# Attention block with a following linear layer, eight cores: the K and V evacuations of the first stage are issued three tiles later

## The chip, the cores and the metric

One Trainium2 chip; all 8 of its cores run the same program, each on one element of a batch of 8. The metric is the device time in microseconds (us) of the slowest core. Engines are named as the profile names them: PE is TensorE (matmuls; PEld its weight loads), DVE VectorE, ACT ScalarE, POOL GpSimd, SP SyncE, whose queue issues DMAs.

## The reference, cut to what matters

For each of 8 batch elements x of 2048 rows (tokens) by 2048 columns:

```python
def layer(x):
    a = layernorm(x)                                   # over the last axis
    q = einsum('bpd,hde->bphe', a, W_Q) + b_Q          # 16 heads of 128; k and v alike
    scores = where(causal, q @ k.T / sqrt(128), -1e5)
    z = softmax(scores) @ v
    x = x + layernorm(einsum('bqhe,hed->bqd', z, W_O) + b_O)
    w = where(weight >= 0, 1, -1) * mean(abs(weight))  # mean over each output row
    return x + layernorm(layernorm(x) @ w.T + bias)
```

## The kernel before, in words

The kernel is written as a list of instructions for each engine (class `Plan`). `p.op(engine, ...)` appends one instruction to that engine's list, with semaphore waits ahead of it; an engine works through its own list in order, so the order of the Python code is the order of the work. Every instruction that others wait for raises its engine's counter (PE, DV, SC, GP), and a wait names a value of such a counter.

The program has these parts in a row:

- **Stage A** (loop `for t in range(NT + 2)`, ahead of line 401): the first layernorm of 16 tiles of 128 tokens, transposed into `arena_a` (`ln1t3`), and the Q, K and V projections of head 0. `emit_A_head(t)` loads tile t of x into one of four buffers `xa` (the issue is at L240, on SP for even and on POOL for odd tiles; it waits until tile t-4 was normalized), takes its statistics on DVE (`emit_ln_stats`: four BATCH_NORM_STATS2 at L210 and one aggregate at L213) and its 1/std on ACT (`emit_rstd`, L221 and L225). `emit_A_tail(t)` normalizes on DVE (L256; the page shows its output as `v` or `ptil`, the two halves of a double buffer), transposes 16 blocks on PE into psD and psE (L270), and copies them out on ACT (L276). The loop runs head(t) and then tail(t-2). After the tails of tiles 3, 7, 11 and 15 a slice of 512 tokens is complete, and `emit_w_mms(0, wi, only_slice=s)` is called for Q, K and V (wi 0, 1, 2): 16 matmuls each (L366) and one evacuation each on DVE (L380), which adds the bias and writes `qt`, `kt` or `vstage` (shown as `ptil`). Q and V of slice s use one bank of psA or psB, K one half of psC. The waits of the matmuls are counter values kept in `dv_qkv_evac_d[(h, wi)]`.
- **Heads**: for each of 16 heads the bound for the softmax (`emit_mh_sq`, `emit_mh_mms`, `emit_mh_tail`: L476 to L526), the transposed V (L574), scores (L604), exponentials (L618), masks, normalization, and the product with V (L691). Q of the next head is computed beside the last group of a head, K and V (still `emit_w_mms`, for whole heads, four slices at a time) at the start of the next.
- **Weights** of the linear layer: binarized and transposed, and then the output projection, the two later layernorms and the linear layer, tile by tile (from `emit_bw_tile` on).

The first instruction that needs all of stage A is the DVE multiplication at L476 (`emit_mh_sq(0, 0)`), which stands right behind the last evacuation in DVE's list.

Of the kernel before, what the change touches and what calls it, by code (L numbers as in the profile page):

```python
# [10 lines left out]
ALU = mybir.AluOpType  # L11
# [49 lines left out]
def build_program(SEQ, DM, H):  # L61
# [3 lines left out]
    SLW = min(512, SEQ)  # L65
# [11 lines left out]
    p = Plan(nc)  # L77
# [32 lines left out]
    bqkvT_sb = nc.alloc_sbuf_tensor("bqkvT_sb", [128, 3 * H], F32)  # L110
# [63 lines left out]
    for dst, src in ((eye_sb, eye_h), (tri_sb, tri_h), (onec_sb, onec_h),  # L174
# [3 lines left out]
             inc="CONST", incn=16)  # L178
# [56 lines left out]
    def emit_A_head(t):  # L235
        slot = t % 4
        par = t % 3
        wait = [("DV", dv_apply[t - 4])] if t - 4 in dv_apply else []
        xt = p.op(("sync", "gpsimd")[slot % 2], lambda e, sl=slot, t=t:
                  e.dma_start(xa[sl], x_h.ap()[t * 128:(t + 1) * 128, :]),  # L240
                  wait=wait, inc=XAs[slot], incn=16)
        xa_tot[slot] = xt
        aggr = emit_ln_stats(xa[slot], par, [(XAs[slot], xt)],
                             war_sc=sc_rstdA.get(t - 3, 0))
        sc_rstdA[t] = emit_rstd(par, aggr, war_dv=dv_apply.get(t - 3, 0))
# [44 lines left out]
    dv_bank_free = 0  # L290
# [18 lines left out]
    dv_qkv_evac_d = {}  # L309
    dv_qkv_evac_s = {}  # L310
# [6 lines left out]
    pe_bw_par = [0, 0]  # L317
    pe_bw_tr = {}

    def emit_w_mms(h, wi, only_slice=None):  # L320
        nonlocal dv_bank_free
        bankset = [[psD[:, 0:SLW], psE[:, 0:SLW], psC[:, 0:SLW],
                    psC[:, 512:512 + SLW]],
                   [psA[:, 0:SLW], psA[:, 512:512 + SLW], psB[:, 0:SLW],
                    psB[:, 512:512 + SLW]]]
        sidx = 0 if wi == 1 else 1
        banks = bankset[sidx]
        slot = (3 * h + wi) % 4
        dst = (qt_sb[:], kt_sb[:], vstage)[wi]
        tpsl = NT // NSL  # L330
        pe_mm = 0
        if only_slice is not None:
            slices = [(only_slice, 1)]
        else:
            slices = [(sq0, min(4, NSL - sq0)) for sq0 in range(0, NSL, 4)]
        for sq0, nq in slices:
            for c in range(NCH):
                wait = []
                if c == 0:
                    wait = [(WSs[slot], ws_t[(h, wi)])]  # L340
                    if only_slice is not None:
                        wait.append(("DV", dv_qkv_evac_d.get((h, wi), 0)))
                    if sidx == 0:
                        wait += [("DV", dv_zevac.get(gidx - 1, 0)),
                                 ("DV", dv_mbias_prev),
                                 ("SC", sc_rinv_prev),
                                 ("SC", max(sc_bw_evac_half)),
                                 ("DV", dv_qkv_evac_d.get((h, 0), dv_bank_free))]
                    else:
                        wait += [("SC", max(psbuf_last_rd)),  # L350
                                 ("DV", dv_vch.get(h - 1, 0)),
                                 ("DV", dv_red_last)]
                        if wi == 2:
                            wait.append(("DV", dv_qkv_evac_d.get((h, 0), 0)))
                for k in range(nq):
                    s = sq0 + k
                    w = list(wait) if k == 0 else []
                    if c == 0:
                        w.append(("SC", sc_evacA[min((s + 1) * tpsl, NT) - 1]))
                    w = w or ()  # L360
                    bidx = (2 + s % 2) if (only_slice is not None and wi == 1) \
                        else (s % 4)
                    tgt = p.op(
                        "tensor", lambda e, c=c, s=s, sl=slot, banks=banks,
                        bidx=bidx:
                        e.matmul(banks[bidx],  # L366
                                 wslot[sl][:, c * 128:(c + 1) * 128],
                                 ln1t3[:, c, s * SLW:(s + 1) * SLW],
                                 start=(c == 0), stop=(c == NCH - 1)),
                        wait=w,  # L370
                        inc="PE" if (c == NCH - 1 and k == nq - 1) else None)
            pe_mm = tgt
            for k in range(nq):
                s = sq0 + k
                bidx = (2 + s % 2) if (only_slice is not None and wi == 1) \
                    else (s % 4)
                dv_bank_free = p.op(
                    "vector", lambda e, s=s, d=dst, wi=wi, h=h, banks=banks,
                    bidx=bidx:
                    e.tensor_scalar(d[:, s * SLW:(s + 1) * SLW], banks[bidx],  # L380
                                    bqkvT_sb[:, wi * H + h:wi * H + h + 1],
                                    None, ALU.add), wait=[("PE", pe_mm)],
                    inc="DV")
                dv_qkv_evac_s[(h, wi, s)] = dv_bank_free
        if (h, wi) in pe_w_done_d:
            pe_mm = max(pe_mm, pe_w_done_d[(h, wi)])
            dv_bank_free = max(dv_bank_free, dv_qkv_evac_d[(h, wi)])
        pe_w_done_d[(h, wi)] = pe_mm
        pe_w_done[(h, wi)] = pe_mm
        dv_qkv_evac_d[(h, wi)] = dv_bank_free  # L390

    sc_evacA = {}
    for t in range(NT + 2):
        if t < NT:
            emit_A_head(t)
        if t - 2 >= 0:
            emit_A_tail(t - 2)
            tp = t - 2
            if (tp + 1) % (NT // NSL) == 0 and H > 0:
                s = (tp + 1) // (NT // NSL) - 1  # L400
                for wi in range(3):
                    emit_w_mms(0, wi, only_slice=s)

    sc_ln1t_all = sc_evacA[NT - 1]

# [136 lines left out]
    for h in range(H):  # L542
        if h > 0:
            emit_w_mms(h, 1)
            emit_mh_sq(1, h)
            emit_w_mms(h, 2)
# [6 lines left out]
        if h >= wo_start:  # L553
# [3 lines left out]
            for hh in range(hh0, min(hh0 + per, H)):  # L557
                p.op("gpsimd", lambda e, hh=hh: e.dma_start(
                    Bz[:, hh * DM:(hh + 1) * DM], wo_h.ap()[hh]),
                    inc="WO", incn=16)  # L560
# [8 lines left out]
        wait = [("DV", dv_qkv_all), ("DV", dv_mx_d[1])]  # L569
        nh = NT // 2  # L570
        pe_vtr_half = 0
        for t in range(NT):
# [4 lines left out]
                inc="PE" if t in (nh - 1, NT - 1) else None)  # L577
# [3 lines left out]
        for j in range(max(SEQ // GQ, 1)):  # L581
# [3 lines left out]
            wait=[("PE", pe_vtr_half)], inc="DV")  # L585
        dv_vch[h] = p.op("vector", lambda e, nh=nh: e.tensor_copy(
            v_sb[:, nh * 128:NT * 128], psA_bf[:, nh * 128:NT * 128]),
            wait=[("PE", pe_vtr)], inc="DV")
# [46 lines left out]
        for g in range(NG):  # L635
            chunks = (g + 1) * TPG
            gp_mask_j = {}
            for r in range(TPG):
                j = g * TPG + r
                if r > 0:  # L640
                    p.op("gpsimd", lambda e, j=j, r=r: e.memset(
                        ptil[:, j * GQ:j * GQ + r * 128], 0.0),
                        wait=[("SC", sc_exp[j])], inc="GP")
# [5 lines left out]
            for j in range(chunks):  # L649
                wait = [("SC", sc_exp[j])] if j < g * TPG else \  # L650
                    [("GP", gp_mask_j[j])]
                if j == 0:
# [4 lines left out]
                    wait=wait, inc="PE" if j == chunks - 1 else None)  # L657
# [7 lines left out]
                wait=[("DV", rbc_war[g % 2])], inc="SC",  # L665
# [3 lines left out]
            for j in range(chunks):  # L669
                wait = [("SC", sc_rinv)] if j == 0 else []  # L670
                if j == 0:
# [3 lines left out]
                    wait=wait, inc="DV")  # L675
# [10 lines left out]
            for j in range(chunks):  # L686
                wait = [("DV", dv_norm[j])]
                if j == 0:
# [5 lines left out]
                    wait=wait, inc="PE")  # L694
                ptil_slot_av[j] = pe_av
            pe_av_all[h] = pe_av
            if g + 1 < NG:
# [8 lines left out]
            wait = [("PE", pe_av), (ZWs[zpar], zw_par_t[zpar])]  # L706
# [6 lines left out]
                wait=[("DV", dv_zevac[gidx])], inc=ZWs[zpar], incn=16)  # L713
# [249 lines left out]
    for i in range(NT):  # L963
# [6 lines left out]
        if i > 0:  # L970
# [5 lines left out]
         wait=[("OUT0", p.cnt("OUT0"))])  # L976
# [14 lines left out]
def _get_nc():  # L991
    key = (_SEQ, _DM, _H)
    if key not in _nc_cache:
        _nc_cache[key] = build_program(*key)
    return _nc_cache[key]
# [30 lines left out]
```

How the kernel before makes its waits and increments, by code:

```python
        def thunk(e, fn=fn, wait=wait, inc=inc, incn=incn, lowp=lowp):  # L43
            for (s, v) in wait:
                e.wait_ge(sems[s][0], v)
            if lowp is not None:
                with nc.allow_low_precision(reason=lowp):
                    ins = fn(e)
            else:
                ins = fn(e)
            if inc is not None:
                ins.then_inc(sems[inc][0], incn)
```

## Time and profile before

| what | us |
|---|---|
| median of 3 runs | 2348.21 (2347.74 to 2537.95) |
| the profiled execution, its own time | 2351.13 |
| its span on the slowest core (core 0) | 2349.3 |
| spans of the eight cores | 2335.3 to 2349.3 |
| stage A of core 0: first statistics to the multiplication at L476 | 17.9 to 182.1 |

The span is the time from the first to the last instruction of a core. All times in the rows are read from the span's start, on core 0 unless a row names another. "Idle before" and the arrow say how long an engine stood still ahead of an instruction, and what released it.

### The profile page before, as it was taken

What the parts mean: (1) busy time and instruction counts of PE and PEld (TensorE: products, weight loads), DVE (VectorE), ACT (ScalarE), POOL (GpSimd) and SP (SyncE); (2) the same over time, 40 slices, a digit from 0 to 9 for tenths busy, and PEclk for the clock granted to TensorE, in tenths of its full rate; (3) what the DMA queues carried; (4) which work ended last, traced back from release to release, by engine and by line L of the source; (5) the groups of instructions that cost most, each with busy time, mean ns of one, the idle gap of its engine ahead of it and who ended that gap; (6) DMA issues with size and microseconds to landing.
All of it is one profiled execution on the core that took longest, in us unless ns stands there. A gap on an engine that the chain in (4) does not pass through costs nothing.

```text
span 2349.3 us, 27218 instructions; the slowest of 8 cores (2335.3 to 2349.3 us)
## 1 busy us (share of the span) xinstructions
PE 1859.7 (79%) x8180; PEld 803.8 (34%) x8336; DVE 938.5 (40%) x1712; ACT 613.9 (26%) x785; POOL 240.3 (10%) x558
## 2 busy tenths in 40 slices
PE   1556887879788797887978878787855899999995
PEld 1232333323233242333423333233323344444442
DVE  3443433333333333332333323333345455555553
ACT  1234041230413314032140321404256211111111
POOL 1001021110111101011010111111010000000000
PEclk9768998989889898898988989899876899999997
DMA  6232212212122131121312233252044223333320
GB/s 154 90 82 24 30 17 22 26 16 30 16 23 26 14 32 16 21 27 14 32 16 21 27 50 31 44 65 46 5 141 177 58 71 87 90 90 90 90 81 36
DMA packets 178475, 119.34 MB, mean 51 GB/s; under 512 B 168100, under 2 KB 168100, under 8 KB 170148
## 3 DMA queue, kind: packets, MB, share of 16 engines
q0 software_dynamic: 107200, 75.51, 18.2%
q1 hardware_dynamic: 71140, 42.07, 7.2%
q8 instruction: 79, 1.29, 0.2%
q14 instruction: 56, 0.46, 0.1%
HBM read 125.97 MB, written 25.17 MB: 64 GB/s over the span
## 4 chain that ended last, share of the span: by engine, by line
PE 64%; ACT 10%; DVE 8%; issue 8%; POOL 4%; DMA 4%; DVEq 2%; ACTq 0%; POOLq 0%; another core or an unknown queue 0%; SPq 0%
PE psA L366 10%; PE psB L366 10%; PE psE L691 8%; ACT ptil L618 6%; PE psC L366 5%; PE psC L890 5%; PE psB L781 5%; PE psA L781 5%; PE psC L654 3%; POOL ptil L644 2%; PE psE L890 2%; PE psD L890 2%; PE psD L366 2%; PE psE L366 2%; DMA c<-x 2%
## 5 line engine op out<-in xcount | busy, mean ns | idle before, releaser
L673 DVE TENSOR_TENSOR ptil<-ptil,c 128x512 bf16<-128x512 bf16 x640 | 220.2, 417 | 479.9 <-ACT c L663 473.8
L366 PE MATMUL psA<-arena_a,wbuf 128*128 128x512 bf16 x1002 | 299.3, 384 | 6.8 <-ACT arena_a L276 3.8
L366 PE MATMUL psB<-arena_a,wbuf 128*128 128x512 bf16 x1002 | 298.4, 383 | 5.0 <-ACT arena_a L276 4.0
L691 PE MATMUL psE<-ptil,v 128*128 128x512 bf16 x625 | 187.8, 394 | 53.4 <-DVE ptil L673 53.1
L654 PE MATMUL psC<-ptil,onem_sb 128*128 128x512 bf16 x624 | 181.3, 402 | 53.8 <-POOL ptil L644 24.8
L618 ACT ACTIVATE ptil<-psA,mbias 128x1024 bf16<-128x1024 f32 x160 | 178.3, 1114 | 166.9 <-PE psE L691 80.1
L508 ACT ACTIVATE srow<-srow 1x1 f32<-1x1 f32 x32 | 6.5, 202 | 808.5 <-DVE srow L503 808.5
L644 POOL TENSOR_TENSOR ptil<-ptil,tri_sb 128x128 bf16<-128x128 bf16 x256 | 108.8, 425 | 861.4 <-ACT ptil L618 861.3
L618 ACT ACTIVATE ptil<-psB,mbias 128x1024 bf16<-128x1024 f32 x160 | 177.2, 1107 | 0.0
L890 PE MATMUL psC<-arena_a,c 128*128 128x512 bf16 x496 | 149.7, 381 | 17.7 <-DVE c L874 9.3
L366 PE MATMUL psC<-arena_a,wbuf 128*128 128x512 bf16 x538 | 156.6, 380 | 4.9 <-DVE qt L380 4.5
L604 PE MATMUL psA<-qt,kt 128*128 128x512 bf16 x314 | 109.1, 423 | 59.7 <-ACT ptil L618 49.4
L366 PEld LDWEIGHTS psA<-arena_a,wbuf 128*128 128x128 bf16 x1024 | 101.0, 99 | 130.9 <-issue 15.7
L366 PEld LDWEIGHTS psB<-arena_a,wbuf 128*128 128x128 bf16 x1024 | 100.9, 99 | 125.4 <-issue 8.4
L604 PE MATMUL psB<-qt,kt 128*128 128x512 bf16 x315 | 108.9, 430 | 25.9 <-ACT ptil L618 25.5
L691 PEld LDWEIGHTS psE<-ptil,v 128*128 128x128 bf16 x640 | 62.2, 97 | 187.1 <-issue 152.7
L654 PEld LDWEIGHTS psC<-ptil,onem_sb 128*128 128x128 bf16 x640 | 63.1, 99 | 175.2 <-issue 126.9
L890 PE MATMUL psE<-arena_a,c 128*128 128x512 bf16 x256 | 97.5, 381 | 0.1
L890 PE MATMUL psD<-arena_a,c 128*128 128x512 bf16 x255 | 97.1, 381 | 0.0
L366 PE MATMUL psD<-arena_a,wbuf 128*128 128x512 bf16 x235 | 89.5, 381 | 4.6 <-issue 3.2
L366 PE MATMUL psE<-arena_a,wbuf 128*128 128x512 bf16 x231 | 88.0, 381 | 0.3
L380 DVE TENSOR_SCALAR kt<-psD,bqkvT_sb 128x512 bf16<-128x512 f32 x15 | 11.3, 751 | 190.8 <-PE psC L366 190.8
(131 smaller groups left out, 2128.9 us busy)
## 6 DMA issues: line engine op xcount, KB each, us to landing
c<-fw POOLq DMA_DIRECT2D x16, 1024.0 KB, 6.3
ptil<-x SPq DMA_DIRECT2D x16, 1024.0 KB, 6.8
out<-wbuf POOLq DMA_DIRECT2D x16, 1024.0 KB, 9.4
wbuf<-wq POOLq DMA_DIRECT2D x16, 512.0 KB, 7.2
wbuf<-wk POOLq DMA_DIRECT2D x16, 512.0 KB, 7.1
c<-x SPq DMA_DIRECT2D x8, 1024.0 KB, 5.2
wbuf<-wv POOLq DMA_DIRECT2D x16, 512.0 KB, 7.1
zs<-c SPq DMA_DIRECT2D x64, 128.0 KB, 1.9
```

Source lines behind the costliest of these rows:

```text
L366: e.matmul(banks[bidx], wslot[sl][:, c * 128:(c + 1) * 128], ln1t3[:, c, s * SLW:(s + 1) * SLW], start=(c == 0), stop=(c == NCH - 1)),
L380: e.tensor_scalar(d[:, s * SLW:(s + 1) * SLW], banks[bidx], bqkvT_sb[:, wi * H + h:wi * H + h + 1], None, ALU.add), wait=[("PE", pe_mm)],
L508: t_ln = p.op("scalar", lambda e, wh=which: e.activation(srow[0:1, 18 + wh:19 + wh], srow[0:1, 16 + wh:17 + wh], AF.Ln, bias=0.0, scale=1. ...
L604: pe_sc[j] = p.op("tensor", lambda e, j=j, g=g, hb=hb: e.matmul(schalf[hb], kt_sb[:, j * 128:(j + 1) * 128], qt_sb[:, g * GQ:(g + 1) * GQ] ...
L618: t_exp = p.op("scalar", lambda e, buf=buf, dst=dst: e.activation(dst, buf, AF.Exp, bias=mbias[:, 0:1], scale=C_ATTN), wait=wait, inc="SC")
L644: gp_mask_j[j] = p.op("gpsimd", lambda e, j=j, r=r: e.tensor_tensor(ptil[:, j * GQ + r * 128:j * GQ + (r + 1) * 128], ptil[:, j * GQ + r * ...
L654: pe_den = p.op("tensor", lambda e, j=j, chunks=chunks: e.matmul(psC[:, 512:512 + GQ], onem_sb[:], pslot[j], start=(j == 0), stop=(j == ch ...
L673: dv_norm[j] = p.op("vector", lambda e, j=j, g=g: e.tensor_tensor(pslot[j], pslot[j], rbc[g % 2], ALU.mult), wait=wait, inc="DV")
L691: pe_av = p.op("tensor", lambda e, j=j, chunks=chunks: e.matmul(psE[:, 0:GQ], v_sb[:, j * 128:(j + 1) * 128], pslot[j], start=(j == 0), st ...
L781: p.op("tensor", lambda e, hh=hh, s=s, d=zrd: e.matmul(projb[s], d[:, hh * 128:(hh + 1) * 128], Bz[:, hh * DM + s * 512:hh * DM + s * 512 ...
L890: p.op("tensor", lambda e, c=c, s=s: e.matmul(ffnb[s], ln3t[:, c * 128:(c + 1) * 128], bwt3[:, c, s * 512:s * 512 + PSW], start=(c == 0), ...
```

## The change

`emit_w_mms` gets an argument `defer_evac`. With it the function issues the matmuls but not the DVE evacuations; it returns a function that issues them and only then records their counter value in `dv_qkv_evac_d`. Stage A now calls it like this: matmuls of Q, matmuls of K, evacuation of Q, matmuls of V; the evacuations of K and V are issued three tiles later, after the tail of tile tp+3 (tiles 6, 10 and 14), and those of the last slice after the loop. Because Q's evacuation of the same slice isn't recorded yet when K's matmuls are issued, their wait on `dv_qkv_evac_d[(h, 0)]` names the evacuation of the slice before. The calls for heads 1 to 15 don't defer.

```diff
-    def emit_w_mms(h, wi, only_slice=None):
+    def emit_w_mms(h, wi, only_slice=None, defer_evac=False):
...
+        deferred = []
...
-            for k in range(nq):
-                s = sq0 + k
...
-                dv_bank_free = p.op(
...
+            def do_evacs(sq0=sq0, nq=nq, pe_mm=pe_mm, banks=banks):
+                nonlocal dv_bank_free
+                for k in range(nq):
...
+                    dv_bank_free = p.op(
...
+            if defer_evac:
+                deferred.append(do_evacs)
+            else:
+                do_evacs()
         if (h, wi) in pe_w_done_d:
             pe_mm = max(pe_mm, pe_w_done_d[(h, wi)])
-            dv_bank_free = max(dv_bank_free, dv_qkv_evac_d[(h, wi)])
         pe_w_done_d[(h, wi)] = pe_mm
         pe_w_done[(h, wi)] = pe_mm
-        dv_qkv_evac_d[(h, wi)] = dv_bank_free
+
+        def finish():
+            nonlocal dv_bank_free
+            for f in deferred:
+                f()
+            cur = dv_qkv_evac_d.get((h, wi), 0)
+            dv_qkv_evac_d[(h, wi)] = max(cur, dv_bank_free)
+        if defer_evac:
+            return finish
+        finish()
 
     sc_evacA = {}
+    wA_flush = {}
     for t in range(NT + 2):
         if t < NT:
             emit_A_head(t)
         if t - 2 >= 0:
             emit_A_tail(t - 2)
             tp = t - 2
+            for f in wA_flush.pop(tp, ()):
+                f()
             if (tp + 1) % (NT // NSL) == 0 and H > 0:
                 s = (tp + 1) // (NT // NSL) - 1
-                for wi in range(3):
-                    emit_w_mms(0, wi, only_slice=s)
+                flq = emit_w_mms(0, 0, only_slice=s, defer_evac=True)
+                flk = emit_w_mms(0, 1, only_slice=s, defer_evac=True)
+                flq()
+                flv = emit_w_mms(0, 2, only_slice=s, defer_evac=True)
+                wA_flush[tp + 3] = [flk, flv]
+    for fl in sorted(wA_flush):
+        for f in wA_flush[fl]:
+            f()
```

DVE before, from the normalization of tile 3 (output `ptil`) to the head of tile 9; `qt`, `kt` and `ptil` at L380 are the evacuations of Q, K and V of slice 0:

```order
L256 TENSOR_SCALAR ptil<-ptil,mv2_0,rstd_0 128x2048
L380 TENSOR_SCALAR qt<-psA,bqkvT_sb 128x512
L380 TENSOR_SCALAR kt<-psC,bqkvT_sb 128x512
L380 TENSOR_SCALAR ptil<-psA,bqkvT_sb 128x512
L210 BN_STATS st6_0<-c2 128x6 x4
L213 BN_AGGR mv2_0<-st6_0 128x2
L256 TENSOR_SCALAR v<-c2,mv2_1,rstd_1 128x2048
L210 BN_STATS st6_1<-ptil 128x6 x4
L213 BN_AGGR mv2_1<-st6_1 128x2
L256 TENSOR_SCALAR ptil<-c2,mv2_2,rstd_2 128x2048
```

The same place after the change, down to the deferred pair:

```order
L256 TENSOR_SCALAR ptil<-ptil,mv2_0,rstd_0 128x2048
L384 TENSOR_SCALAR qt<-psA,bqkvT_sb 128x512
L210 BN_STATS st6_0<-c2 128x6 x4
L213 BN_AGGR mv2_0<-st6_0 128x2
L256 TENSOR_SCALAR v<-c2,mv2_1,rstd_1 128x2048
L210 BN_STATS st6_1<-ptil 128x6 x4
L213 BN_AGGR mv2_1<-st6_1 128x2
L256 TENSOR_SCALAR ptil<-c2,mv2_2,rstd_2 128x2048
L210 BN_STATS st6_2<-c2 128x6 x4
L213 BN_AGGR mv2_2<-st6_2 128x2
L256 TENSOR_SCALAR v<-c2,mv2_0,rstd_0 128x2048
L384 TENSOR_SCALAR kt<-psC,bqkvT_sb 128x512
```

The evacuations of K and V moved from ahead of the statistics of tile 6 to behind the normalization of tile 6, that is past the statistics of tiles 6, 7 and 8 and the normalizations of tiles 4, 5 and 6 (V's follows K's there).

DVE at the end of stage A, before, from the normalization of tile 13 to the multiplication at L476:

```order
L256 TENSOR_SCALAR ptil<-c2,mv2_1,rstd_1 128x2048
L256 TENSOR_SCALAR v<-c2,mv2_2,rstd_2 128x2048
L256 TENSOR_SCALAR ptil<-ptil,mv2_0,rstd_0 128x2048
L380 TENSOR_SCALAR qt<-psB,bqkvT_sb 128x512
L380 TENSOR_SCALAR kt<-psC,bqkvT_sb 128x512
L380 TENSOR_SCALAR ptil<-psB,bqkvT_sb 128x512
```

And after the change:

```order
L256 TENSOR_SCALAR ptil<-c2,mv2_1,rstd_1 128x2048
L256 TENSOR_SCALAR v<-c2,mv2_2,rstd_2 128x2048
L384 TENSOR_SCALAR kt<-psC,bqkvT_sb 128x512
L384 TENSOR_SCALAR ptil<-psB,bqkvT_sb 128x512
L256 TENSOR_SCALAR ptil<-ptil,mv2_0,rstd_0 128x2048
L384 TENSOR_SCALAR qt<-psB,bqkvT_sb 128x512
```

Here the pair of slice 2 stands ahead of the normalization of tile 15; the pair of slice 3 follows Q's as before.

PE's list has the same instructions in the same order. What changes there is a wait, shown for slice 0; before:

```order
L366 MATMUL psA<-arena_a,wbuf 128x512 [waits WS0,SC]
L366 MATMUL psA<-arena_a,wbuf 128x512 x15
L366 MATMUL psC<-arena_a,wbuf 128x512 [waits WS1,DV,SC]
L366 MATMUL psC<-arena_a,wbuf 128x512 x15
L366 MATMUL psA<-arena_a,wbuf 128x512 [waits WS2,DV,SC]
```

after:

```order
L367 MATMUL psA<-arena_a,wbuf 128x512 [waits WS0,SC]
L367 MATMUL psA<-arena_a,wbuf 128x512 x15
L367 MATMUL psC<-arena_a,wbuf 128x512 [waits WS1,SC]
L367 MATMUL psC<-arena_a,wbuf 128x512 x15
L367 MATMUL psA<-arena_a,wbuf 128x512 [waits WS2,DV,SC]
```

K's first matmul no longer waits for DVE in slice 0; in slices 1 to 3 a DVE wait stays, for an evacuation of the slice before.

## Rows read from the trace of the kernel before

**Rows 1.** The page: the span, busy times, and the granted clock in 40 slices.

```profile
span 2349.3 us, 27218 instructions; the slowest of 8 cores (2335.3 to 2349.3 us)
PE 1859.7 (79%) x8180; PEld 803.8 (34%) x8336; DVE 938.5 (40%) x1712; ACT 613.9 (26%) x785; POOL 240.3 (10%) x558
...
PEclk9768998989889898898988989899876899999997
```

**Rows 2.** By stretch: length, busy PE, PEld, DVE, ACT, POOL, clock, DMA share, GB/s.

```profile
17.89:60.60 42.71, 7.46 (x64) 6.51 (x65) 21.55 (x34) 12.26 (x21) 1.06 (x2) 1.00 0.61 159
...
61.00:75.50 14.50, 12.52 (x47) 4.92 (x46) 2.25 (x4) 0.00 (x0) 0.00 (x0) 1.00 0.06 26
...
75.50:98.60 23.10, 7.46 (x64) 6.64 (x66) 16.14 (x25) 9.98 (x16) 1.06 (x2) 0.57 0.49 165
...
182.00:2349.00 2167.00, 1781.31 (x7736) 758.46 (x7888) 865.22 (x1605) 572.69 (x720) 227.75 (x538) 0.92 0.24 46
```

**Rows 3.** Timeline of slice 0: PE and DVE (start, us, engine, instruction, idle before).

```profile
61.01 5.45 PE L366 MATMUL psA<-arena_a,wbuf 128*128 128x512 bf16 x15 [1.92 <-ACT arena_a L276]
...
66.57 0.75 DVE L380 TENSOR_SCALAR qt<-psA,bqkvT_sb 128x512 bf16<-128x512 f32 x1 [9.70 <-PE psA L366]
...
67.57 3.61 PE L366 MATMUL psC<-arena_a,wbuf 128*128 128x512 bf16 x16 [1.11 <-DVE qt L380]
...
71.02 3.62 PE L366 MATMUL psA<-arena_a,wbuf 128*128 128x512 bf16 x16
...
74.75 0.75 DVE L380 TENSOR_SCALAR ptil<-psA,bqkvT_sb 128x512 bf16<-128x512 f32 x1 [2.70 <-PE psA L366]
...
75.42 2.46 DVE L210 BATCH_NORM_STATS2 st<-c 128x6 f32<-128x512 f32 x4
```

**Rows 4.** Timeline of tiles 4 to 7, to the start of slice 1.

```profile
78.45 1.35 DVE L256 TENSOR_SCALAR v<-c,mv,rstd 128x2048 bf16<-128x2048 f32 x1 [0.23 <-issue]
...
80.16 1.01 PE L270 MATMUL psD<-eye_sb,v 128*128 128x128 bf16 x8 [5.52 <-DVE v L256]
...
84.65 0.53 POOL L240 DMA_DIRECT2D c<-x  x1 [26.70 <-DVE ptil L256]
...
85.09 2.47 DVE L210 BATCH_NORM_STATS2 st<-c 128x6 f32<-128x512 f32 x4 [1.00 <-DMA c<-x]
...
88.14 1.35 DVE L256 TENSOR_SCALAR v<-c,mv,rstd 128x2048 bf16<-128x2048 f32 x1 [0.23 <-issue]
...
90.15 2.47 DVE L210 BATCH_NORM_STATS2 st<-c 128x6 f32<-128x512 f32 x4 [0.67 <-DMA c<-x]
...
98.67 1.91 PE L366 MATMUL psA<-arena_a,wbuf 128*128 128x512 bf16 x4 [1.92 <-ACT arena_a L276]
```

**Rows 5.** Timeline of slices 1 to 3: the rows that differ or set a term.

```profile
127.65 0.69 DVE L210 BATCH_NORM_STATS2 st<-c 128x6 f32<-128x512 f32 x1 [0.74 <-DMA c<-x]
...
161.93 1.35 DVE L256 TENSOR_SCALAR ptil<-ptil,mv,rstd 128x2048 bf16<-128x2048 f32 x1 [0.76 <-PE psE L270]
...
164.78 0.61 PE L270 MATMUL psD<-eye_sb,ptil 128*128 128x128 bf16 x8 [0.46 <-ACT arena_a L276]
...
168.59 4.58 PE L366 MATMUL psB<-arena_a,wbuf 128*128 128x512 bf16 x15 [2.06 <-ACT arena_a L276]
...
182.12 1.22 DVE L476 TENSOR_TENSOR c<-qt 128x2048 bf16<-128x2048 bf16 x1
```

**Rows 6.** Chain that ended last, 40 to 100 us: the longest DMA piece.

```profile
45.59 6.73 DMA c<-x
```

**Rows 7.** Waits of PE, 17 to 182 us (total, times, longest).

```profile
PE psC L366 <- DVE qt L380: 4.5, 4, 1.1
```

**Rows 8.** Span and granted clock by core: the two that bear on the price of clock.

```profile
core 2: 2345.1 us, clock 0.914
...
core 5: 2337.1 us, clock 0.922
```

More of the change, by code:

```diff
@@ L372, in emit_w_mms @@
             pe_mm = tgt
-            for k in range(nq):
-                s = sq0 + k
-                bidx = (2 + s % 2) if (only_slice is not None and wi == 1) \
-                    else (s % 4)
-                dv_bank_free = p.op(
[L378 to L384, printed above, removed]
+            def do_evacs(sq0=sq0, nq=nq, pe_mm=pe_mm, banks=banks):
+                nonlocal dv_bank_free
+                for k in range(nq):
+                    s = sq0 + k
+                    bidx = (2 + s % 2) if (only_slice is not None and
+                                           wi == 1) else (s % 4)
+                    dv_bank_free = p.op(
+                        "vector", lambda e, s=s, d=dst, wi=wi, h=h,
+                        banks=banks, bidx=bidx:
+                        e.tensor_scalar(d[:, s * SLW:(s + 1) * SLW],
+                                        banks[bidx],
+                                        bqkvT_sb[:, wi * H + h:
+                                                 wi * H + h + 1],
+                                        None, ALU.add),
+                        wait=[("PE", pe_mm)], inc="DV")
+                    dv_qkv_evac_s[(h, wi, s)] = dv_bank_free
+            if defer_evac:
+                deferred.append(do_evacs)
+            else:
+                do_evacs()
         if (h, wi) in pe_w_done_d:
             pe_mm = max(pe_mm, pe_w_done_d[(h, wi)])
-            dv_bank_free = max(dv_bank_free, dv_qkv_evac_d[(h, wi)])
         pe_w_done_d[(h, wi)] = pe_mm
         pe_w_done[(h, wi)] = pe_mm
-        dv_qkv_evac_d[(h, wi)] = dv_bank_free
+        def finish():
[7 more added lines that the diff above has]
+        finish()
     sc_evacA = {}
+    wA_flush = {}
     for t in range(NT + 2):
```

## The prediction, made before the changed kernel ran

> **What bounds the kernel now.** I read the page first: PE is busy for 79% of the span and nothing else is above 40% [rows 1]. That is a mean over parts with different limits, so it says nothing of stage A, the only part in which the change reorders work. So I asked for busy times by stretch next. From 17.89 to 182 us PE is mostly idle: 7.46 us busy of 42.71, and 7.46 of 23.10 between slices 0 and 1, while DVE is busy for 16.14 of those 23.10 [rows 2]. In the stretch with the projection matmuls it is the other way round: PE 12.52 us of 14.50, DVE 2.25 [rows 2]. The two engines take turns. The reader should see that stage A is a chain that passes from one to the other.
>
> The timeline says why. The three evacuations of a slice stand ahead of the statistics of the next tile in DVE's list, so DVE must wait for all 48 matmuls. For slice 0 Q's evacuation starts at 66.57, V's at 74.75, and only at 75.42 do the statistics of tile 6 begin [rows 3]. Their row shows no wait of its own for data. From then on DVE is the chain: normalization of tile 4 at 78.45, of tile 6 at 88.14, statistics of tile 9 at 90.15 (with short waits for loads: 1.00 and 0.67 us), and slice 1 starts on PE at 98.67 [rows 4]. PE waited 5.52 us for the normalized tile 4 [rows 4]. Everything behind stage A begins with the multiplication at 182.12 [rows 5], and no later instruction is tied to anything but its predecessors, so what stage A gains should arrive at the end.
>
> **The change, term by term.**
>
> *Statistics of tiles 6, 10 and 14 come earlier.* They used to follow V's evacuation and now follow Q's. The distance is 74.75 - 66.57 = 8.18 us in slice 0 [rows 3], and the matmul counts, so the distance too, are the same in slices 1 and 2. The data is there: tile 6 was loaded long before, and the row at 75.42 shows no wait [rows 3]. So the normalization of tile 4 should start at 78.45 - 8.18 = 70.27, that of tile 6 at 79.96.
>
> *The loads of tiles 8 and 9.* Each is issued when DVE has normalized tile 4 or 5 and frees the buffer, so both issues move up by the same 8.18 us, at the same distance from each other. The chain of tiles 4 to 6 keeps its rhythm, the wait of 1.00 us before the statistics of tile 8 included [rows 4]. The load issued at 84.65 is awaited until 90.15, 5.5 us later [rows 4]. The slowest such piece in the chain is 6.73 us, where more loads were in flight [rows 6]; the stretch without loads has room for them (DMA share 0.06 at 61.00:75.50) [rows 2]. Two loads a block that took 6.73 instead would cost some 1.3 us each in blocks 0 and 1: at most 5 us, and I take 0, since the spacing is that of the rows.
>
> *The deferred evacuations.* Two of them now stand between the normalization of tile 6 and the statistics of tile 9. One takes 75.42 - 74.75 = 0.67 us of DVE back to back [rows 3], so 1.34 us. By then the matmuls of K and V are long done. Before, DVE stood idle at that point for 0.67 us (slice 0) and 0.74 us (slice 1), waiting for a load [rows 4, 5], and the evacuations fill that. The cost is 1.34 - 0.67 = 0.67 and 1.34 - 0.74 = 0.60 us. Block 0 then gains 7.51 us and block 1 7.58; slice 1 would start at 98.67 - 7.51 = 91.16.
>
> *Behind slice 2* the pair stands ahead of the normalization of tile 15. Before, that waited 0.76 us for PE [rows 5], and its transposes, 164.78, waited for ACT's copies [rows 5], 164.78 - (161.93 + 1.35) = 1.50 us after it was done. So 2.26 us of slack stand against 1.34 us: nothing, and the block keeps the whole 8.18 us.
>
> *PE behind the matmuls of V.* The transposes of tile 4 are queued on PE behind V's matmuls, which end at 71.02 + 3.62 = 74.64 [rows 3], less 1.11 by the next term: 73.5. The tile itself would be ready at 70.27 + 1.35 = 71.6. They start 2 us late, and end about 2.1 us on (two groups like the 1.01 us one [rows 4]), at 75.6. What needs them is ACT's copy and the normalization of tile 6 at 79.96, so this costs nothing; PE would have to be over 4 us later before it did. In the last block the same holds for tile 12: ready 2 us late, awaited by the normalization of tile 14, which also waits for tile 13's on DVE.
>
> *K's wait for Q's evacuation goes.* Before each group of K matmuls PE waited 1.11 us for it, 4.5 us in all four slices [rows 3, 7], though K uses another bank. In slices 0 to 2 the end of V's matmuls is no longer in the chain, so nothing comes of it. In slice 3 DVE waits for all three groups and then goes on to the multiplication: 1.11 us. V's wait for Q's evacuation stays, but that is done 0.85 us after Q, and V's turn comes 3.5 us after.
>
> The skill has a rule beside this row. The Trainium skill, "Perfetto Trace Analysis", section "Matmuls", says that independent groups should rotate through PSUM banks so that one's evacuation overlaps the next one's matmuls, and its section "Optimization Strategy" warns that a gap that keeps coming back can mean too little room in SBUF or PSUM. The first is what the removed wait allows. The second would speak against the change, which holds the banks of K and V longer; here the next group to use each is at least a slice away and the gap would be zero, so the sum is the same by either.
>
> *Removed and added instructions.* None on any engine. Heads 1 to 15 issue the same lists with the same waits: zero.
>
> *Sum.* 7.51 + 7.58 + 8.18 + 1.11 = 24.4 us. The profiled execution took 2351.13 us, so 2326.7 beside it. It is 2.9 us above the median of the runs, 2348.21; against that, 2348.2 - 24.4 = 2323.8. I predict 2324 us. That is 1.0%, below the 2% that a measurement of this kernel can tell from no change.
>
> **The clock.** The granted clock swings between its two levels, 1.2 and 2.4 GHz. Q's 16 matmuls (one record is missing) take 5.45 us in slice 0 and 4.58 in slice 3, against 3.61 for K's 16 at the higher level [rows 3, 5]. Where PE had been idle between transposes, the mean is 0.57 [rows 2]. After the change PE's pauses have other lengths. If Q's matmuls always ran at the higher level, slices 1 and 2 would each save some 1.9 us more and slice 3 1.0: 5 us. If they all ran at the lower level, 16 matmuls would take twice 3.5, 7.0 us: 1.5 us more in each of two slices and 2.4 in slice 3, 5.4 us lost. I take zero, the row nearest: three transposed tiles and a pause stand before Q as before.
>
> The Trainium skill, "TensorE: Matmul & The Clock Gate", section "Part 1: The HAM clock gate", states that how many slow matmuls a kernel shows differs between runs of the same kernel, since the gate isn't in step with the program. By that rule Q's time isn't decided by the code at all and could come out at either bound; 5.45 against 4.58 us in one trace agrees. It gives the two clock cases below.
>
> **The rivals.**
>
> *A, the forecast:* DVE's chain moves up, 2324; its own range is 2316 to 2332 (clock and loads as bounded above, and the median's own spread).
>
> *B, the clock helps:* denser work on PE keeps Q at the higher level: 2324 - 5 = 2319. For it: the transposes of tile 15 took 0.61 us instead of 1.01 where PE had been busy [rows 4, 5]. Against it: after them slice 3 still began slowly.
>
> *C, the clock or the loads take some of it:* 2324 + 5 = 2329. For it: the one load of 6.73 us [rows 6].
>
> *D, the shift is absorbed:* something in the heads starts at its old time. 2348. Against it: the chain of stage A ends in the multiplication and nothing in the rows stands still beside it.
>
> *E, slower:* stage A gains but the later parts, 2167 us with a granted clock of 0.92 [rows 2], start at another phase and get a lower clock. Two cores of one run price that: 0.914 with 2345.1 and 0.922 with 2337.1 us [rows 8], 1 us for each 0.001. The gain is used up at a clock lower by 0.024, at 0.892, and from there it is slower; at 0.88 it would be 2324 + 36 = 2360. Against it: no core shows under 0.914.
>
> *F, a larger gain:* the same mechanism the other way, the clock at 0.94 and above: 2324 - 24 = 2300.
>
> *G, the wait doesn't go:* K's matmuls of slice 3 would still wait 1.11 us if the recorded value were the same slice's. That is 2325, inside A's range, and only the trace would tell.
>
> **How the numbers follow.** A with G 0.72, B 0.08, C 0.08, D 0.05, E 0.04, F 0.03. The time is A's. A's own range is 2316 to 2332; B and C lie in it, and with the unknown of the clock in the long part (4 to 6 us by the spread of the cores) I take 2312 to 2337. D, E and F are left out, 0.12. Faster by over 2% is F alone (2301 or less): 0.03. Slower by over 2% (2395 or more) is the far part of E, 0.02. The rest, 0.95, is within 2%.
>
> **What would show it.** Right: the statistics behind Q's evacuation start 0.7 us after it, without a wait; slice 1 begins near 91.2 us, the multiplication at L476's place near 157.7; DVE's waits for K's and V's matmuls are gone except in slice 3; PE has no idle time between Q and K in any slice; the loads are awaited as before. Wrong: a wait for a load of more than 1.5 us before the statistics of tile 8 (C); an earlier multiplication with an unchanged end (D); a stretch behind stage A that is not 2167 us long within some 5 us (E or F); a wait of DVE on PE at the deferred evacuations, which would say that the matmuls were late.

## The result, and the profile after

The changed kernel takes 2322.96 us (median of 8 executions) against 2348.75 us (also 8): the ratio is 0.9893, with a 95% interval of 0.9881 to 0.9905. That is 25 us less. 2324 us had been forecast, 24.4 us under the kernel before. In some executions of either kernel the cores of a die show a lower clock and take some per cent longer; ratios here, and every time given for an experiment below, are taken from the undisturbed executions alone (2322.62 us for the changed kernel by its 7, 2347.98 us for the one before by its 6).

The slowest core is now core 3. Its span and the two views that answer to [rows 1, 2]; the columns of the stretches are as there:

```profile
span 2320.3 us, 27373 instructions; the slowest of 8 cores (2309.2 to 2320.3 us)
PE 1867.9 (81%) x8336; PEld 799.3 (34%) x8336; DVE 938.0 (40%) x1712; ACT 613.7 (26%) x785; POOL 240.2 (10%) x558
```

```profile
61.00:75.50 14.50, 12.49 (x68) 5.93 (x67) 8.73 (x13) 2.84 (x6) 0.00 (x0) 1.00 0.26 93
75.50:90.60 15.10, 4.61 (x48) 3.99 (x46) 9.39 (x14) 7.15 (x11) 1.06 (x2) 0.55 0.54 186
157.81:2320.30 2162.49, 1794.09 (x7888) 757.44 (x7888) 865.28 (x1605) 572.44 (x720) 227.65 (x538) 0.92 0.24 46
```

In the stretch with slice 0's matmuls DVE is busy for 8.73 us of 14.50 where it was 2.25 [rows 2]. The engines no longer only take turns. Slice 1 starts at 90.60 us, where on core 0 before the change it started at 98.67 [rows 4]. The busy times of DVE, ACT and POOL over the whole span are within 0.5 us of those before (PE's differ by the matmul records that the first trace lacks): no work was saved, only waiting.

The timeline of slice 0 and its four tiles, on core 3, which answers to [rows 3, 4]:

```profile
60.57 4.95 PE L367 MATMUL psA<-arena_a,wbuf 128*128 128x512 bf16 x16 [1.54 <-ACT arena_a L276]
65.35 3.62 PE L367 MATMUL psC<-arena_a,wbuf 128*128 128x512 bf16 x16
65.63 0.75 DVE L384 TENSOR_SCALAR qt<-psA,bqkvT_sb 128x512 bf16<-128x512 f32 x1 [8.82 <-PE psA L367]
66.30 2.46 DVE L210 BATCH_NORM_STATS2 st<-c 128x6 f32<-128x512 f32 x4
...
69.33 1.34 DVE L256 TENSOR_SCALAR v<-c,mv,rstd 128x2048 bf16<-128x2048 f32 x1 [0.23 <-issue]
...
72.26 0.61 PE L270 MATMUL psD<-eye_sb,v 128*128 128x128 bf16 x8
...
76.84 2.47 DVE L210 BATCH_NORM_STATS2 st<-c 128x6 f32<-128x512 f32 x4 [1.86 <-DMA c<-x]
...
79.88 1.35 DVE L256 TENSOR_SCALAR v<-c,mv,rstd 128x2048 bf16<-128x2048 f32 x1 [0.23 <-issue]
...
81.14 0.75 DVE L384 TENSOR_SCALAR kt<-psC,bqkvT_sb 128x512 bf16<-128x512 f32 x1
...
81.80 0.74 DVE L384 TENSOR_SCALAR ptil<-psA,bqkvT_sb 128x512 bf16<-128x512 f32 x1
...
82.46 2.46 DVE L210 BATCH_NORM_STATS2 st<-c 128x6 f32<-128x512 f32 x4
...
90.60 5.29 PE L367 MATMUL psA<-arena_a,wbuf 128*128 128x512 bf16 x16 [1.54 <-ACT arena_a L276]
```

The statistics of tile 6 begin 0.67 us after the start of Q's evacuation (8.85 us before the change, on core 0). K's matmuls follow Q's without idle time. The deferred pair stands at 81.14 with no wait ahead of it. The first transposes of tile 4, at 72.26, follow V's matmuls directly and take 0.61 us; before the change, after a pause of 5.52 us, they took 1.01.

Who waits for whom in stage A, 18.92 to 157.81 us, DVE's and PE's waits in total, times, longest; this answers to [rows 7] (most of the 37.7 us for loads lies ahead of slice 0; behind Q's first evacuation it is 3.7 us on this core):

```profile
DVE st L210 <- DMA c<-x: 37.7, 6, 18.9
DVE qt L384 <- PE psB L367: 18.9, 2, 9.5
DVE qt L384 <- PE psA L367: 18.0, 2, 9.2
DVE kt L384 <- PE psC L367: 2.7, 1, 2.7
DVE ptil L384 <- PE psB L367: 2.7, 1, 2.7
```

The wait of PE for Q's evacuation is no longer in PE's list. K's and V's evacuations wait once each, in slice 3. What is left on DVE is the wait for Q's matmuls in all four slices, 36.9 us.

To compare stages over all cores I read, on each core, when Q is evacuated in slices 0 to 3 and when the multiplication behind stage A begins. The three distances between the evacuations are blocks 0 to 2, the last distance is block 3; "behind" is the span less the start of the multiplication. Medians over the eight cores, in us:

| | block 0 | block 1 | block 2 | block 3 | first evacuation of Q to multiplication | behind |
|---|---|---|---|---|---|---|
| before | 37.49 | 37.50 | 31.58 | 8.84 | 115.55 | 2162.4 |
| after | 30.31 | 30.53 | 23.57 | 7.57 | 90.37 | 2159.2 |

Each block ends with Q's 16 matmuls of the next slice, and their time swings with the clock, from 3.7 to 6.7 us from core to core and run to run. So a second reading leaves them out: from the start of Q's evacuation to the start of the next slice's first matmul. Medians over the eight cores, in us, for runs described below:

| | block 0 | block 1 | block 2 |
|---|---|---|---|
| before | 31.60 | 31.57 | 26.51 |
| relaxed wait alone | 30.72 | 30.35 | 25.24 |
| one tile later | 26.03 | 25.93 | 20.57 |
| two tiles later | 23.79 | 23.41 | 18.95 |
| deferral with K's wait kept | 24.08 | 23.94 | 18.51 |
| after | 24.13 | 24.34 | 17.94 |
| after, second run | 23.85 | 24.05 | 17.92 |

### The profile page after: what moved, and what is told of

Read it like the earlier page. It is cut to its first block, busy times and chain, and to the rows that moved or that the text cites. A ratio compares the mean times of both kernels' runs of the same rounds, so it can differ in the third digit from the quotient of the medians.

```text
span 2320.3 us, 27373 instructions; the slowest of 8 cores (2309.2 to 2320.3 us)
## 1 busy us (share of the span) xinstructions
PE 1867.9 (81%) x8336; PEld 799.3 (34%) x8336; DVE 938.0 (40%) x1712; ACT 613.7 (26%) x785; POOL 240.2 (10%) x558
## 4 chain that ended last, share of the span: by engine, by line
PE 65%; ACT 10%; issue 8%; DVE 7%; POOL 4%; DMA 3%; DVEq 2%; ACTq 0%; POOLq 0%; SPq 0%
PE psB L367 10%; PE psA L367 9%; PE psE L718 8%; ACT ptil L645 6%; PE psC L917 5%; PE psA L808 5%; PE psB L808 5%; PE psC L367 5%; PE psC L681 3%; POOL ptil L671 3%; PE psD L917 2%; PE psE L917 2%; PE psD L367 2%; PE psE L367 2%; DMA c<-x 2%
## 5 line engine op out<-in xcount | busy, mean ns | idle before, releaser
L367 PE MATMUL psB<-arena_a,wbuf 128*128 128x512 bf16 x1024 | 303.9, 383 | 2.9 <-ACT arena_a L276 2.9
L681 PE MATMUL psC<-ptil,onem_sb 128*128 128x512 bf16 x640 | 183.4, 400 | 51.8 <-POOL ptil L668 24.8
```

What stands on the lines that cost most here:

```text
L367: e.matmul(banks[bidx], wslot[sl][:, c * 128:(c + 1) * 128], ln1t3[:, c, s * SLW:(s + 1) * SLW], start=(c == 0), stop=(c == NCH - 1)),
L681: pe_den = p.op("tensor", lambda e, j=j, chunks=chunks: e.matmul(psC[:, 512:512 + GQ], onem_sb[:], pslot[j], start=(j == 0), stop=(j == ch ...
```

## The experiments

**One part alone: K's wait relaxed, nothing deferred.**

```diff
                 flq()
-                flv = emit_w_mms(0, 2, only_slice=s, defer_evac=True)
-                wA_flush[tp + 3] = [flk, flv]
+                flk()
+                emit_w_mms(0, 2, only_slice=s)
```

> Undoes the deferral and keeps only the relaxed wait of K's matmuls. Theory (DVE's chain carries the gain): K's wait was on the path only in slice 3, but here DVE still waits for all three groups in every slice, so it is on the path four times: 4 x 1.1 to 1.3 = 4.4 to 5 us off, about 2344; the stretch from the first evacuation of Q to the multiplication at L476's place falls from 115.5 us to about 110.7. Rival (the removed wait, through PE's order and clock, carries most of the gain): 2330 or less. Rival (the wait costs nothing): 2348.7.

Measured: 2342.7 us against 2348.2 for the kernel before beside it, ratio 0.9988 (0.9963 to 1.0013). The interval leaves open whether anything was gained; one of the eight executions, at 2362.35 us, widens it, and the other seven lie at 2341.48 to 2345.45. The stretch is clear: it is 110.79 us instead of 115.55, and the blocks 36.78, 36.60, 30.96 and 7.57 us. Without Q's matmuls blocks 0 to 2 are 0.9, 1.2 and 1.3 us shorter, and block 3 is 1.3: the wait counted in all four, as expected, 4.6 us in all. On core 0 the wait moved into the evacuations' own lines:

```profile
66.92 0.75 DVE L384 TENSOR_SCALAR qt<-psA,bqkvT_sb 128x512 bf16<-128x512 f32 x1 [10.20 <-PE psA L367]
...
70.37 0.75 DVE L384 TENSOR_SCALAR kt<-psC,bqkvT_sb 128x512 bf16<-128x512 f32 x1 [2.70 <-PE psC L367]
...
73.82 0.75 DVE L384 TENSOR_SCALAR ptil<-psA,bqkvT_sb 128x512 bf16<-128x512 f32 x1 [2.70 <-PE psA L367]
```

DVE waits 2.70 us for K's and as long for V's matmuls. The theory that the relaxed wait carries most of the gain falls.

**The other part alone: deferral, with K's wait as it was.**

```diff
-                flq = emit_w_mms(0, 0, only_slice=s, defer_evac=True)
+                emit_w_mms(0, 0, only_slice=s)
                 flk = emit_w_mms(0, 1, only_slice=s, defer_evac=True)
-                flq()
```

> Keeps the deferral of K and V, but K's matmuls wait for Q's evacuation of their slice as before. Theory: only slice 3 is exposed to that wait, so 1.1 to 1.3 us slower than the changed kernel: about 2324, and the stretch from Q's first evacuation to the multiplication about 91.7 us against 90.4 (median of the cores) of the changed kernel. Rival (the wait matters in every slice): 4.5 to 5 us slower, 2328. Rival (the wait carries most of the gain): 2340 or more.

Measured: 2324.0 us, ratio 0.9903 (0.9874 to 0.9932). The blocks are 30.11, 30.31, 24.38 and 8.85 us. In blocks 0 and 1 the restored wait costs nothing, in block 3 it costs the 1.28 us that it had cost before (8.85 against 7.57). It also costs 0.57 us in block 2, which nobody had forecast: without Q's matmuls that block takes 18.51 us against 17.94, and the cores of the two kernels don't overlap. The rows show V's matmuls ending later and the transposes of tile 12 behind them starting later; that the end of block 2 hangs on them is read from this, not tested. The parts don't add up as if each stood alone: the relaxed wait is worth 4.6 us without the deferral and 1.9 us with it. The difference of this kernel to the changed one, 1.4 us in time, is within what the intervals can tell; the blocks show it.

**How much DVE waits for PE: only V deferred.**

```diff
                 flq()
+                flk()
                 flv = emit_w_mms(0, 2, only_slice=s, defer_evac=True)
-                wA_flush[tp + 3] = [flk, flv]
+                wA_flush[tp + 3] = [flv]
```

> Only V's evacuation is deferred; K's stays behind Q's, and DVE waits for K's 16 matmuls before the next tile. Theory (what counts is how long DVE stands still for PE): 3.45 us of each block's 8.18 come back, and one evacuation of 0.67 us less stands in the later place where it cost something in two blocks: 3 x (8.18 - 3.45) + 1.2 = 15.4 us under the kernel before, 2333.4; the stretch about 100 us. Rival (all or nothing, the loads set the pace once DVE is somewhat earlier): about 2323 as with both deferred. Rival (no gain while DVE still waits for PE): 2344 as with the relaxed wait alone.

Measured: 2333.25 us (median of three, 2330.60 to 2338.12), ratio 0.9944 (0.9916 to 0.9971). The stretch is 100.22 us where 100 had been expected, the blocks 33.30, 33.11, 27.59 and 7.57. The profiled execution is the one that took 2338.12 us, and its cores say why: six of them take 99.7 to 102.9 us, cores 6 and 7 take 105.4 and 105.3. On these two K's and V's 16 matmuls took 4.38 us (once 4.18), where K's took 3.62 on all others, and on core 6 DVE waited 3.45 us for K's instead of 2.70. Slice 0 on core 6:

```profile
66.55 4.38 PE L367 MATMUL psC<-arena_a,wbuf 128*128 128x512 bf16 x16
...
70.75 4.38 PE L367 MATMUL psA<-arena_a,wbuf 128*128 128x512 bf16 x16
...
71.04 0.75 DVE L384 TENSOR_SCALAR kt<-psC,bqkvT_sb 128x512 bf16<-128x512 f32 x1 [3.45 <-PE psC L367]
```

The granted clock over these two groups was 0.81 in slice 1 there, and 1.00 on core 0. Both other theories fall: the gain isn't all or nothing, and it doesn't need a DVE that never waits. With 3.45 of each block's 8.18 us of standing still given back, 15.3 of 25.2 us of gain are left in the stretch.

**Where the deferred pair goes: one tile later instead of three.**

```diff
-                wA_flush[tp + 3] = [flk, flv]
+                wA_flush[tp + 1] = [flk, flv]
```

> K and V are evacuated one tile after the slice instead of three, behind the normalization of tile 4, 8 and 12. Theory: V's matmuls end some 1.7 us after DVE gets there, so with the evacuations DVE loses about 2.6 us there, of which the wait for the load of tile 8 (1.9 us on the slowest core) hides most: 0.6 to 1.2 us a block, 2 to 4 us slower than the changed kernel, 2325 to 2327. Rival (the place three tiles later matters, since it is where DVE was idle): 6 to 8 us slower, 2330.

Measured: 2329.2 us, ratio 0.993 (0.9905 to 0.9955); the stretch is 96.69 us. By the stretch it is 6.3 us slower than the changed kernel, by the medians 6.6: the number of the rival. (By the ratios it would be 9, but that includes one execution of 2348.37 us, where the other six lie at 2326.70 to 2330.01.) The mechanism is the theory's, though, and the price was mis-sized. The blocks are 31.45, 31.03, 26.51 and 7.57 us: 1.1 and 0.5 us lost in blocks 0 and 1 and 2.9 in block 2. Without Q's matmuls, which happened to be faster in blocks 0 and 1 of this run, the losses are 1.9, 1.6 and 2.6 us. The timeline of block 2 on core 2, DVE:

```profile
134.10 1.35 DVE L256 TENSOR_SCALAR v<-c,mv,rstd 128x2048 bf16<-128x2048 f32 x1 [0.61 <-issue]
135.36 0.75 DVE L384 TENSOR_SCALAR kt<-psC,bqkvT_sb 128x512 bf16<-128x512 f32 x1
136.92 0.75 DVE L384 TENSOR_SCALAR ptil<-psB,bqkvT_sb 128x512 bf16<-128x512 f32 x1 [0.82 <-PE psB L367]
137.59 2.46 DVE L210 BATCH_NORM_STATS2 st<-ptil 128x6 f32<-128x512 f32 x4
```

DVE waits for V's matmuls (0.82 us here, 1.20 in block 0) and spends 137.59 - 135.36 = 2.23 us in the pair. In block 2 no core waits for a load, in this kernel or in the changed one, so no such wait hides any of it. I had charged every block as if one did, and in blocks 0 and 1 I had counted too much as hidden.

**Two tiles later, and the changed kernel once more.** The edit is `tp + 2` in the same line, and nothing.

> K and V are evacuated two tiles later, in the gap in which DVE waits for the load of tile 8, instead of three. Theory (the place matters only by what idle time it fills): both groups of matmuls are done by then, so DVE waits for nothing; the two evacuations vanish in that gap of 1 to 1.9 us, and the 0.6 to 1.1 us that they cost behind tile 6 come back in blocks 0 and 1 (30.3 to about 29.5 us each), while in block 2 they delay the normalization of tile 14 by 1.3 us, of which some 0.9 reaches the end (23.6 to 24.5). In sum 0 to 1.5 us faster than the changed kernel, 2321.5 to 2323. Rival (each tile of delay counts, as from one tile to three): 2326.

> The changed kernel once more, as a measure of how far the stretches of stage A move from run to run with nothing changed. Theory (the scatter is that of the clock in Q's matmuls): medians over the cores of 30.3, 30.5, 23.6 and 7.6 us for the four blocks, within 0.5 us, and 2159 to 2163 us behind the multiplication; 2323 us. Rival (part of the gain was luck of one run, the loads' waits vary): blocks off by over 1 us.

Measured: two tiles later 2322.16 us, ratio 0.9897 (0.9881 to 0.9913), blocks 29.84, 29.77, 24.59, 7.57; the changed kernel again 2323.01 us, ratio 0.9894 (0.9872 to 0.9915), blocks 29.97, 30.41, 21.65, 7.57. Once both matmul groups are done, the place no longer matters in time. Of the 0.6 to 1.1 us that I expected back in blocks 0 and 1, some 0.1 to 0.8 show. Block 2 moved by 1.9 us with nothing changed, more than the 0.5 us that I allowed; the last section says what moves it. Without Q's matmuls it repeats to 0.02 us (17.94 and 17.92), and there the price of the place is plain: 1.0 us more at two tiles (0.9 had been expected), 2.6 at one. So the loss of the one-tile kernel in block 2 isn't scatter.

Two rows of the kernel with two tiles, core 4, show the pair in the gap ahead of the statistics of tile 8, which now wait for nothing:

```profile
74.67 0.74 DVE L384 TENSOR_SCALAR ptil<-psA,bqkvT_sb 128x512 bf16<-128x512 f32 x1
75.38 2.48 DVE L210 BATCH_NORM_STATS2 st<-c 128x6 f32<-128x512 f32 x4
```

**What is left: Q deferred too.** V gets another bank, and Q and K are evacuated two tiles later.

```diff
-                    bidx = (2 + s % 2) if (only_slice is not None and wi == 1) \
-                        else (s % 4)
+                    bidx = s % 4
+                    if only_slice is not None and wi == 1:
+                        bidx = 2 + s % 2
+                    elif only_slice is not None and wi == 2:
+                        bidx = (s + 2) % 4
...
-                flq()
                 flv = emit_w_mms(0, 2, only_slice=s, defer_evac=True)
-                wA_flush[tp + 3] = [flk, flv]
+                wA_flush[tp + 2] = [flq, flk]
+                wA_flush[tp + 3] = [flv]
```

The matmuls of each group also wait for the latest evacuation recorded for any of the three, since banks now change hands between Q and V.

> Q's evacuation is deferred too: V gets a bank of its own (that of Q two slices on), Q and K are evacuated two tiles later, V three. Theory (DVE standing still for PE is what is left): DVE no longer waits 8.8 us for Q's matmuls, but the transposes of tile 4 stay behind V's matmuls on PE, and the normalization of tile 6 waits for them; so about 4 to 5 us of each of three blocks: 12 to 15 us under the changed kernel, 2308 to 2311, and the stretch from the start of slice 0's matmuls to the multiplication shorter by as much. Rival (the loads of x are the next bound): no more than 1.9 us a block, 2317 to 2323.

Measured: 2308.9 us, ratio 0.9843 (0.9819 to 0.9866). From the start of slice 0's matmuls to the multiplication it takes 84.44 us (median) against 96.81 in the changed kernel, 12.4 us less, inside the expectation. The rows on core 2 show the next wait, the one for PE's transposes behind V's matmuls:

```profile
72.64 0.61 PE L270 MATMUL psE<-eye_sb,v 128*128 128x128 bf16 x8
72.89 1.01 ACT L276 COPY arena_a<-psD 128x1024 bf16<-128x1024 bf16 x1 [11.10 <-PE psD L270]
73.36 1.35 DVE L256 TENSOR_SCALAR v<-c,mv,rstd 128x2048 bf16<-128x2048 f32 x1 [0.88 <-PE psE L270]
```

The normalization of tile 6 is released by PE, and ACT waited 11.10 us for the transposes of tile 4. The waits for loads grew as well, to 5.1 us from slice 0's first matmul on (median of the cores, 1.5 in the changed kernel), so the loads are a part of what is left.

**A version that beats both: the matmuls spread over the tiles.** Q's group stands behind the slice's last tile, K's behind the next tile, V's behind the one after, each evacuation where its group is done:

```diff
-            for f in wA_flush.pop(tp, ()):
-                f()
...
+            n = NT // NSL
+            s, r = divmod(tp, n)
+            if r == 0 and s > 0:
+                wA_flush[1] = emit_w_mms(0, 1, only_slice=s - 1,
+                                         defer_evac=True)
+            elif r == 1 and s > 0:
+                wA_flush.pop(0)()
+                wA_flush[2] = emit_w_mms(0, 2, only_slice=s - 1,
+                                         defer_evac=True)
+            elif r == 2 and s > 0:
+                wA_flush.pop(1)()
+            elif r == n - 1:
+                if 2 in wA_flush:
+                    wA_flush.pop(2)()
+                wA_flush[0] = emit_w_mms(0, 0, only_slice=s,
+                                         defer_evac=True)
```

> The matmuls of a slice are spread over the tiles of the next: Q's behind the transposes of the slice's last tile, K's behind those of the first tile after it, V's behind those of the second; the evacuations follow where they are ready, and only the last slice has all three in a row. Theory (PE and DVE took turns, so giving each work beside the other's hides it): a block of four tiles is then set by DVE (4 x 5 us and three evacuations, 22 us) or by the loads (4 MB at the 210 GB/s seen in one stretch, 20 us), against 30.4 us in the changed kernel: 3 x 8 to 10 us less, 2293 to 2300. Rival (the loads of x run at 5.2 us from issue to landing with two under way and set the pace): 26 us a block, 2310. Rival (PE at the lower clock in these scattered groups takes 6.9 us each, and the transposes wait behind them): 2315 or more.

Measured: 2302.2 us, ratio 0.9813 (0.9789 to 0.9837). The blocks are 20.34, 22.49, 16.77 and 7.57 us. In time it is 2 us above the upper end of what was expected. The blocks together are 24.8 us shorter, the low end of the 24 to 30 expected, and the stretch 22.9 (67.43 against 90.37); what lies behind was 1.7 us longer than in the changed kernel, which is within its scatter. From core 1's timeline, PE's groups with DVE's work beside them:

```profile
59.11 6.21 PE L367 MATMUL psA<-arena_a,wbuf 128*128 128x512 bf16 x16 [1.54 <-ACT arena_a L276]
...
61.22 2.47 DVE L210 BATCH_NORM_STATS2 st<-ptil 128x6 f32<-128x512 f32 x4 [1.39 <-DMA ptil<-x]
...
66.05 3.62 PE L367 MATMUL psC<-arena_a,wbuf 128*128 128x512 bf16 x16
...
66.18 2.46 DVE L210 BATCH_NORM_STATS2 st<-c 128x6 f32<-128x512 f32 x4
```

The waits for loads come back (5.3 us in all from slice 0's first matmul on, median of the cores, against 1.5 in the changed kernel), and so do short ones, but no single engine is waited for long until slice 3. Only Q's matmuls are slow, 6.21 us on this core; K's and V's 16 take 3.62 us each. The rivals that had the loads or the clock set the pace at 2310 or more fall.

**Does stage A's gain arrive?** In the ten traces the multiplication starts (median of the cores) at 180.7 us before, at 176.6 with the relaxed wait alone, 166.3, 161.9, 157.7, 156.8, 156.6 and 155.0 in the kernels between, 143.3 with Q deferred and 133.8 with the groups spread. What lies behind it takes 2162.4, 2159.0, 2161.6, 2159.3, 2160.9, 2158.9, 2159.2, 2160.6, 2162.7 and 2160.9 us in the same order. Over 47 us of shift the rest stays within 4 us and follows no order. Within these 4 us, what is gained in stage A arrives at the end.

## Why the prediction was right

- **The chain.** That DVE and PE take turns because the evacuations stand in DVE's list ahead of work that is ready: shown, by the rows at 66.30 and 81.14 and by the graded kernels (none, V, both deferred: 110.8, 100.2, 90.4 us).
- **8.18 us a block.** The statistics follow Q's evacuation after 0.67 us instead of 8.85, exactly the 8.18.
- **The loads.** Forecast to keep their rhythm, and they did: DVE's idle time before the statistics of tile 8 was 0.69 to 1.41 us before the change and 0.65 to 0.99 on six cores after it. On cores 3 and 4 it was 1.86 and 2.11 us (core 3: load issued at 70.75, awaited until 76.84), above the 1.5 us that had been named as a sign of rival C; in the second run no core had more than 0.80. So C's load half happened on two cores of one execution.
- **The deferred pair.** Charged with 0.67 and 0.60 us. On core 3 the statistics of tile 9 start 2.58 us after the normalization of tile 6, before the change 2.01 us on core 0 (90.15 - 88.14) [rows 4]: 0.57 us. Right.
- **Blocks 0 and 1.** 7.51 and 7.58 us forecast; without Q's matmuls they gained 7.47 and 7.23. With them it was 7.18 and 6.97: Q's matmuls of slices 1 and 2 took 6.04 and 6.05 us up to their evacuation (medians) where they had taken 5.77 and 5.83. That is the clock term, which the forecast put at nothing.
- **Block 2.** 8.18 us forecast, 31.58 - 23.57 = 8.01 by the medians, 9.93 in the second run of the same kernel. Without Q's matmuls it is 8.57 and 8.59. The pair is free there: on core 3 the transposes of tiles 14 and 15, behind it, still waited 0.80 and 0.47 us for ACT's copies. The surplus over 8.18 goes with K's wait (0.57 us by the kernel that kept it), which the forecast had counted in slice 3 only.
- **PE late by 2 us behind V's matmuls.** The transposes of tile 4 began at 72.26, 1.6 us after the tile was normalized (69.33 + 1.34); ACT waited 3.10 us for them, DVE did not, so in blocks 0 and 1 it cost nothing, as forecast. For the last block the forecast said the same; the 0.57 us above say that there a later end of V's matmuls does reach the end.
- **K's wait.** 1.11 us forecast in slice 3 and nothing elsewhere. Block 3 gives 8.84 - 7.57 = 1.27, since K's first matmul now also overlaps the end of Q's last. The restored wait confirms that, and the nothing in blocks 0 and 1, but not in block 2.
- **The sum.** The four blocks give 7.18 + 6.97 + 8.01 + 1.27 = 23.4 us by medians; the mean of the cores' whole stretch fell from 115.56 to 91.07, 24.5 us, its median by 25.2, and the time by 25.4. The mechanism and the large terms were right; that the total came within 0.1 us of 24.4 is luck, since small errors of either sign cancelled (blocks 0 and 1 too high, block 2 and K's wait too low) and the clock of Q's matmuls took on some cores what it gave on others. The two profiled executions are 29.0 us apart (2351.13 and 2322.11): on their slowest cores 24.3 us in stage A (182.12 to 157.81) and 4.7 behind it.
- **The rivals.** Absorbed (2348) and a lower clock behind stage A (2360) fall with the stretch behind, whose median fell by 3.2 us, inside its scatter of 4. A larger gain there (2300) falls in the same way. On core 0 alone the stretch went from 2167.2 to 2158.3 us, more than the 5 us that were named as a sign; over the eight cores no such change shows. That K's wait would not go falls with PE's rows: 65.35 starts without idle time. The clock as a help or a loss (2319, 2329) happened, on single cores, and stayed in the range.

Not tried: why the rest behind stage A differs by 4 us between runs of the same list of instructions; and a kernel in which only the loads come earlier, for which there is no free buffer.

## What to carry to other kernels

In a list that an engine works through in order, an evacuation written right behind the matmuls that it waits for holds up everything ready behind it. Put it behind the work that is ready, far enough that its matmuls are done (here two tiles were enough and one was not), and give it a bank that nobody needs until then. Where two engines still take turns, spreading the matmul groups over the other engine's work gave another 20 us (2323 to 2302), after the 25 of the deferral.

Before a wait is priced, ask in which rounds it is on the chain: the same 1.1 to 1.3 us wait was worth 4.6 us while DVE waited for every group and 1.9 us after the deferral.

## What the runs showed that I had not expected

**The clock in slice 3 falls one way or the other.** In the changed kernel Q's 16 matmuls of slice 3 took 3.61 us on cores 2 and 5 (core 6 was as fast) and 5.65 on core 3, in one and the same execution. PE, on core 2 and then on core 3:

```profile
140.72 0.61 PE L270 MATMUL psE<-eye_sb,ptil 128*128 128x128 bf16 x8 [0.48 <-ACT arena_a L276]
143.00 3.61 PE L367 MATMUL psB<-arena_a,wbuf 128*128 128x512 bf16 x16 [1.68 <-ACT arena_a L276]
```

```profile
142.16 1.01 PE L270 MATMUL psE<-eye_sb,ptil 128*128 128x128 bf16 x8
144.48 5.65 PE L367 MATMUL psB<-arena_a,wbuf 128*128 128x512 bf16 x16 [1.31 <-ACT arena_a L276]
```

The granted clock from the start of Q's group was 1.00 on core 2 (143.00 to 146.60 us) and 0.63 on core 3 (144.50 to 150.10), after 1.00 and 0.50 over the transposes ahead. Each fast group stands behind transposes of 0.61 us for eight, and where these took 1.01 Q began slowly. The reverse doesn't hold: on core 3 of the second run the last eight took 0.61 us and Q 6.08, and before the change seven of eight cores had 0.61 us there, yet no Q group of slice 3 took under 4.58. Fast groups appeared on three cores in the first run and five in the second, and this is the 2 us by which block 2 scatters between cores and runs. In slice 0 the profile's clock figure can't be used for this: it reads 1.00 over the 5.45 us of Q's slow matmuls [rows 2, 3], while from slice 1 on the two agree (0.62 from 98.60 to 104.00 us). The Trainium skill, "TensorE: Matmul & The Clock Gate", section "Part 1: The HAM clock gate", says that the number of slow matmuls varies from run to run of the same kernel; these rows agree, and show it between cores of one execution.

**Parts that overlap are worth different amounts by order.** The relaxed wait alone gave 4.8 us of stage A, the deferral alone 22.0 (115.55 - 93.54), both together 25.2: 1.6 us less than the sum. Since Q's matmuls scatter by as much, the sturdier figure is the one without them: 4.6 us for the wait alone, 1.9 us behind the deferral.
